# Layer 0's batch ends spread over 40 steps with roots by GpSimd; layer 1's tokens made inside layer 0 and its scan placed at the last value products

## The reference, cut to what matters

```
layer 0 attention (16 heads of 8, per batch):
  scores = (q k' + c2p + p2c) / scale      # c2p, p2c: by relative position
  out    = softmax(scores) v  @ Wo + bo + xn
  out    = (out - mu) * rsqrt(var + 1e-7) * ln_scale + ln_bias
layer 0 ffn:       xn @ sign(weight)'
layer 1 attention (min-GRU, forward and backward over 512 tokens):
  z = sigmoid(xn Wz + bz);  g = xn Wh + bh
  h_t = (1 - z_t) h_(t-1) + z_t G(g_t);    out = [h_f, h_b] @ W_out + b_out
layer 1 ffn (8 experts, 2 per token, 64 places per expert and group of 512):
  probs = softmax(xn @ w_router); two best experts, place = rank in the group
  dispatch -> gelu(. wi[e]) wo[e] -> combine weighted with probs
```

## Time and profile before

| what | us |
|---|---|
| median of 3 runs | 2280.51 (2279.85 to 2285.18) |
| profiled execution | 2277.15 |
| its span, first to last instruction | 2275.3 |
| PE busy / DVE / ACT / POOL | 1944.4 / 1763.7 / 1430.5 / 1223.2 |
| mean granted TensorE clock | 0.960 of full speed |
| main loop of layer 0, first to last add | 74.5 to 920.9 |
| last value products of layer 0 | 925.2 to 928.8 |
| layer 1's first gate product | 975.4 |
| layer 1's first dispatch mask | 1047.3 |

### The profile page before, as it was taken

One profiled execution on the slowest core, in us unless ns is written; L12 is line 12 of the kernel. 1 busy time (PEld: TensorE's weight loads), 2 busy tenths in 40 slices (PEclk: granted clock), 3 DMA queues, 4 the chain that ended last, 5 costly groups with the idle time before them and its releaser, 6 DMA issues.

```text
span 2275.3 us, 38965 instructions
## 1 busy us (share of the span) xinstructions
PE 1944.4 (85%) x13526; PEld 1473.7 (65%) x13526; DVE 1763.7 (78%) x4099; ACT 1430.5 (63%) x2795; POOL 1223.2 (54%) x1028
## 2 busy tenths in 40 slices
PE   3799898888989898587996999999998468788898
PEld 2566565666666666464683878777876345566797
DVE  7688888888888888457187888888887699873586
ACT  2578777777878777344235666666665257765575
POOL 3777677777777775148053445444543466426400
PEclk9999999999999999789997999999999689999999
DMA  3988788888878786201000000000001000003000
GB/s 105 306 304 303 249 294 274 288 268 278 284 271 281 278 300 227 85 1 35 3 6 1 1 1 1 1 1 1 1 1 31 0 0 1 1 1 98 24 2 38
DMA packets 73877, 264.15 MB, mean 116 GB/s; under 512 B 12273, under 2 KB 32241, under 8 KB 73169
## 3 DMA queue, kind: packets, MB, share of 16 engines
q1 hardware_dynamic: 72304, 254.31, 33.2%
q10 hardware_dynamic: 1376, 7.34, 0.8%
HBM read 140.30 MB, written 121.31 MB: 115 GB/s over the span
## 4 chain that ended last, share of the span: by engine, by line
PE 38%; DVE 8%; ACT 6%; POOL 2%; issue 2%; DMA 0%; POOLq 0%; ACTq 0%; DVEq 0%; SPq 0%
PE PS L157 10%; PE PS L161 7%; PE PS L163 7%; PE PS L162 7%; PE PS L326 7%; ACT AR L167 3%; ACT L167 2%; DVE AR L181 1%; DVE DR L181 1%; DVE PT L181 1%; ACT AR L171 1%; ACT PT L171 1%; DVE AR L185 1%; DVE AR L200 1%; DVE AR L193 1%
## 5 line engine op out<-in xcount | busy, mean ns | idle before, releaser
L167 ACT ACTIVATE AR<-PS,AR 128x512 f32<-128x512 f32 x1008 | 686.6, 688 | 286.8 <-DVE AR L193 178.8
L193 DVE TENSOR_REDUCE AR<-PS 128x1 f32<-128x512 f32 x896 | 616.4, 688 | 119.3 <-PE PS L163 100.5
L326 PE MATMUL PS<-ident,AR 128*128 128x128 f32 x3816 | 584.6, 277 | 86.1 <-ACT AR L171 38.6
L157 PE MATMUL PS<-AR 128*9 128x512 f32 (+8 forms) x4190 | 503.5, 360 | 93.0 <-DVE AR L181 32.9
L326 PEld LDWEIGHTS PS<-ident,AR 128*128 128x128 f32 x3816 | 435.0, 142 | 200.6 <-issue 71.2
L181 POOL TENSOR_TENSOR AR<-AR 128x512 f32<-128x512 f32 (+6 forms) x310 | 380.6, 1244 | 226.9 <-DVE AR L181 97.0
L157 PEld LDWEIGHTS PS<-AR 128*9 128x9 f32 (+5 forms) x4190 | 288.8, 133 | 298.4 <-DVE AR L181 130.1
L171 ACT ACTIVATE AR<-PS 128x512 f32<-128x512 f32 (+3 forms) x612 | 356.4, 587 | 91.8 <-PE PS L326 47.7
L176 POOL TENSOR_SCALAR AR<-AR 128x512 f32<-128x512 f32 x144 | 245.4, 1704 | 293.2 <-DVE AR L1596 219.4
L171 ACT ACTIVATE PT<-PS 128x512 fp32r<-128x512 f32 x320 | 191.5, 599 | 208.3 <-PE PS L326 171.5
L181 DVE TENSOR_TENSOR PS<-PS,AR 128x192 f32<-128x192 f32 (+1 forms) x512 | 201.7, 394 | 118.0 <-PE PS L534 112.0
(11 more groups left out here) (157 smaller groups left out, 3001.9 us busy)
## 6 DMA issues: line engine op xcount, KB each, us to landing
scr<-AR SPq DMA_DIRECT2D x128, 800.0 KB, 4.3
XN<-scr SPq DMA_DIRECT2D x85, 768.0 KB, 6.6
AR<-scr SPq DMA_DIRECT2D x43, 768.0 KB, 6.5
AR<-qsc SPq DMA_DIRECT2D x96, 192.0 KB
qsc<-AR SPq DMA_DIRECT2D x96, 128.0 KB, 3.4
AR<-in_wgu SPq DMA_DIRECT2D x16, 256.0 KB, 3.2
X<-in_x ACTq DMA_DIRECT2D x1, 2048.0 KB, 8.5
AR<-in_wi ACTq DMA_DIRECT2D x1, 2048.0 KB, 8.2
```

What stands on the lines that cost most here:

```text
L157: return pe.e.matmul(out, lhsT, rhs, start=start, stop=stop)
L167: return ac.e.activation(out, in_, func, bias=bias, scale=scale, accum_out=accum)
L193: return dv.e.tensor_reduce(out, in_, AX.X, ALU.max, negate=True)
L326: return pe.e.transpose(out, in_, ident[0:k, 0:k])
```

## The change

Layer 0: the ends get one set of places and three new pieces. Step 41 norms T1, step 44 makes the tokens of the batch before last for layer 1 (XR), step 49 transposes them into B_M, and ScalarE copies them into XT in place of layer 0's own. The root is a power of -0.5 on GpSimd over 8 columns: four for T1, four for the batch before's X. newton3 refines it in three operations. The main loop ends 14 steps earlier, and the last batch's end moves into layer 1's units (END0). Layer 1 has no norm stage: its XN are made by `normed`, four scalings a unit. Its small weights are asked for at the last but one group's value products, wi and wo2 by SP after the last end. The router's products stand in groups of four tiles between units 5 and 13; the choice runs in two parts, 28 tiles in units 12 to 14 and the last 4 in unit 15; the ranks' products stand behind unit 15, the exponential behind the last sigmoid, the normalisation of PROB behind the masks. AR loses 36 columns to NY; waits and counts of layers 2 and 3 are renumbered.

```
+def newton3(dv, y, v, tmp):
+    dv.step(stt(dv, y, tmp, -0.5, tmp, ALU.mult, ALU.mult))
+    dv.settle()
+    dv.step(tt(dv, y, y, v, ALU.mult))
+    dv.settle()
+    return stt(dv, y, y, 1.5, tmp, ALU.add, ALU.mult)
...
-        STEPS0 = 4 * NBH + 28
+        STEPS0 = 4 * NBH + 14
-        AHEAD = {"q": 1, "k": 3, "far": 13, "g0": 15, "v": 35}
+        AHEAD = {"q": 1, "k": 3, "far": 13, "g0": 15, "v": 51}
-        ENDS = [{"heads": 17, "ct": 19, "mo": 29, "sw": 31, "root": 34, "norm": 36, "sum": 38, "last": 48}] * NB
-        ENDS += [{"heads": 14, "ct": 16, "mo": 18, "sw": 19, "root": 21, "norm": 22, "sum": 23, "last": 25}]
+        ENDS = {"heads": 17, "ct": 19, "mo": 29, "stats": 32, "root": 34, "norm": 41, "tokens": 44, "sw": 45, "sum": 47, "xt": 49,
+                "last": 57}
...
+            if 2 <= b < NB and r == ENDS["xt"]:
+                uses.append(("xt", b - 2, 0))
...
+                elif what == "xt":
+                    pe.wait_ge(tn_n, 2 * b + 3)
+                    for q in range(4):
+                        ins = tr(pe, ps[:, q * 128:q * 128 + 128], XR[:, q * 128:q * 128 + 128])
...
                 elif k == 1:
-                    dv.wait_ge(m_mm, number["sw", b, 0] + 1)
-                    tt(dv, X[:, xs, :], ps, X[:, xs, :], ALU.add).then_inc(m_dv, 1)
                     dv.wait_ge(*emptied[number["mo", b, 0]])
                     dv.settle()
                     stats(dv, lmv, lst, T1)
                     dv.settle()
-                    ts(dv, lv, lmv[:, :, 1], 1e-7, None, ALU.add).then_inc(tn_v, 1)
+                    if b:
+                        dv.step(ts(dv, lv[:, 4:8], NMV[:, 4 * b - 4:4 * b, 1], 1e-5, None, ALU.add))
+                    ts(dv, lv[:, 0:4], lmv[:, :, 1], 1e-7, None, ALU.add).then_inc(tn_v, 1)
...
-                    dv.step(newton(dv, ly, lv, ltmp))
+                    w = 8 if b else 4
+                    dv.step(newton3(dv, ly[:, 0:w], lv[:, 0:w], ltmp[:, 0:w]))
...
+                elif k == 3:
+                    dv.wait_ge(m_mm, number["sw", b, 0] + 1)
+                    tt(dv, X[:, xs, :], ps, X[:, xs, :], ALU.add).then_inc(m_dv, 1)
+                elif k == 5:
+                    if b:
+                        done = 6 * min(b + 3, NB)
+                        dv.wait_ge(sp_p, done)
+                        dv.wait_ge(sp_a, done)
+                        dv.settle()
+                        dv.step(dv.e.tensor_copy(NY[:, 4 * b - 4:4 * b], ly[:, 4:8]))
+                        for i in range(4 * b - 4, 4 * b):
+                            ins = ts(dv, XR[:, i % 4 * 128:i % 4 * 128 + 128], X[:, i, :], NMV[:, i, 0:1], ly[:, 4 + i % 4:5 + i % 4],
+                                     ALU.subtract, ALU.mult)
+                        ins.then_inc(tn_n, 1)
...
-                        act(ac, ltmp, lv, ACT.Sqrt).then_inc(tn_q, 1)
+            def root(b):
+                w = 8 if b else 4
+                po.wait_ge(po_init, HALF_0)
+                po.wait_ge(tn_v, b + 1)
+                tt(po, ltmp[:, 0:w], lv[:, 0:w], minus_half[:, 0:w], ALU.pow).then_inc(tn_q, 1)
...
+        LAST = NB - 1
+        END0 = {"heads": 0, "ct": 1, "mo": 2, "stats": 3, "sw": 4, "root": 4, "norm": 5, "sum": 6, "xt": 8, "last": 8, "root7": 9,
+                "norm7": 10, "tr7": 11}
+        ROUTER = {5: (0, 4), 6: (4, 8), 7: (8, 12), 8: (12, 16), 9: (16, 20), 10: (20, 24), 11: (24, 28), 13: (28, 32)}
         def l1_sp(sp):
+            sp.wait_ge(pv_mm, 4 * NB - 1)
...
+            after_l0(sp)
+            for dst, name in ((wi, "wi"), (wo2, "wo2")):
+                sp.e.dma_start(dst, a[name]).then_inc(ld[1], 16)
...
-        def l1_pe(pe):
-            norm_pe(pe, 1, lambda c: 4 + c + 1)
+        def l1_pe(pe, small_mm):
             pe.wait_ge(ld[1], NL1)
-            pe.wait_ge(n_xt, 16)
+            pe.wait_ge(s_ex, 4 * NBH)
+            pe.wait_ge(to_a, 4 * NBH)
...
+            for u in range(16):
+                unit(u)
+                for what, b, g in (("heads", LAST, 3), ("ct", LAST, 0), ("mo", LAST, 0), ("sw", LAST, 0), ("xt", LAST - 1, 0)):
+                    if u == END0[what]:
+                        small_mm((what, b, g))
+                if u in ROUTER:
+                    tokens((ROUTER[u][1] - 1) // 4)
+                    for i in range(*ROUTER[u]):
+                        ins = mm(pe, PS[:, 7 if i >= 4 * LAST else 6, i * 8:i * 8 + 8], XT[:, i * 128:i * 128 + 128], router, True, True)
...
+                if u % 2 and u >= 3:
+                    scan_out(u // 2 - 1)
+                if u == END0["tr7"]:
...
+                        ins = tr(pe, PS[:, 7, q * 128:q * 128 + 128], XN[:, 4 * LAST + q, :])
...
+            trail()
             scan_out(NB - 1)
...
+            def normed(b):
+                dv.settle()
+                for i in range(4 * b, 4 * b + 4):
+                    ins = ts(dv, XN[:, i, :], X[:, i, :], NMV[:, i, 0:1], NY[:, i:i + 1], ALU.subtract, ALU.mult)
+                ins.then_inc(xn_dv, 1)
...
+            ROUTE = {12: ((0, first),), 13: ((1, first),), 14: ((2, first),), 15: ((0, last), (1, last), (2, last))}
             for u in range(16):
                 gate(u)
                 if u:
                     scan(u - 1)
                 if u % 2 and u >= 3:
                     scan_out(u // 2 - 1)
-                route(u)
+                for k, sl in ROUTE.get(u, ()):
+                    route(k, sl)
+                if u < LAST:
+                    normed(u)
...
             scan(15)
+            counted()
             scan_out(7)
```

More of the change, by code:

```diff
@@ L419, in program @@
             order += small(u)
+        order += [("heads", NB - 1, 3), ("ct", NB - 1, 0), ("mo", NB - 1, 0), ("sw", NB - 1, 0), ("xt", NB - 2, 0)]
         number, emptied, n_ac, n_dv = {}, [], 0, 0
@@ L588, in l0_pe @@
                     pv(G, r // 2)
+            return small_mm
         def l0_dv(dv):
@@ L927, in l0_po @@
                     split(b + 1, k // 2, k % 2)
-                if b >= 1 and r == ENDS[b]["sum"]:
+                if 1 <= b < NB and r == ENDS["root"]:
+                    root(b - 1)
+                if 1 <= b < NB and r == ENDS["sum"]:
                     tail(b - 1)
+            return root, tail
         def l0_sp(sp):
@@ L1038, in after_l0 @@
             en.wait_ge(p_w, 2 * NBH)
+            en.wait_ge(to_a, 4 * NBH)
+            en.wait_ge(s_ex, 4 * NBH)
+            en.wait_ge(pv_mm, 4 * NB)
         A1 = Arena(nc, AR, ar_at)
         names1 = ["wz_f", "wh_f", "wz_b", "wh_b"]
+        H_, A_ = [A1.take(512) for _ in range(4)], [A1.take(512) for _ in range(3)]
+        PRI, PROB = A1.take(NT, 8), A1.take(NT, 8)
+        assert 2 * 2048 <= A1.top
         w1 = [A1.take(128) for _ in names1]
@@ L1047, in program @@
         router, trile, iota, rev = A1.take(8), A1.take(128), A1.take(64), A1.take(8)
[L1048 to L1051 removed]
+        assert A1.top <= 4 * 2048 and 4 * NB % 2 == 0 and PTN == 6
+        ones128, v7, tmp7 = A1.take(128), A1.take(4), A1.take(4)
         L, L2, E1, E2, W_ = (A1.take(NT, 8) for _ in range(5))
         m8, s8 = A1.take(NT), A1.take(NT)
[L1054 removed]
+        Z0, *ZG = [A1.take(512) for _ in range(6)]
         Z_, G_ = [Z0, *ZG[:2]], ZG[2:]
         zg_at = A1.top - 5 * 512
[L1057 removed]
+        assert A1.top <= PTN * 2048
+        wi, wo2 = A1.take(8, 512), A1.take(8, 4, 128)
         XIN = A1.take(8, 8, 64)
@@ new lines, in route, with counted @@
+                    first_max(E2[:, sl], L2[:, sl], sl).then_inc(rt_dv, 1)
+            def counted():
+                dv.wait_ge(rt_mm, 3)
+                dv.wait_ge(rt_dv, 2)
+                dv.settle()
+                ps = PS[:, 7, :].rearrange("p (k n e) -> p k n e", k=2, e=8)
+                dv.step(tt(dv, E1, E1, ps[:, 0], ALU.mult))
+                dv.step(tt(dv, E2, E2, ps[:, 1], ALU.mult))
+                dv.settle()
+                dv.step(tt(dv, PRI, E1, E2, ALU.max))
+                dv.settle()
+                ts(dv, PRI, PRI, -1.0, None, ALU.add).then_inc(rt_dv, 1)
@@ L1283, in l1_dv @@
                     scan_out(u // 2 - 1)
-                route(u)
+                for k, sl in ROUTE.get(u, ()):
+                    route(k, sl)
+                if u < LAST:
+                    normed(u)
+                if u == END0["heads"]:
+                    heads_out(LAST, 3)
+                if u == END0["mo"]:
+                    tail(LAST, 0)
+                if u == END0["stats"]:
+                    tail(LAST, 1)
+                if u == END0["norm"]:
+                    tail(LAST, 2)
+                    tail(LAST, 3)
+                    tail(LAST, 5)
+                if u == END0["last"]:
+                    tail(LAST, 4)
+                    dv.settle()
+                    ts(dv, v7, NMV[:, 4 * LAST:NT, 1], 1e-5, None, ALU.add).then_inc(tn_v, 1)
+                if u == END0["norm7"]:
+                    dv.wait_ge(tn_v, NB + 1)
+                    dv.wait_ge(tn_q, NB + 1)
```

(11 more changed lines are left out.)

280 lines of the change are left out of this document (140 added, 140 removed).

## The result

The changed kernel takes 2268.68 us (median of 4 runs, 2266.0 to 2271.58) where the kernel before, on the same chip, takes 2280.18: a ratio of 0.9945, interval 0.9924 to 0.9966. It is 11.5 us faster; 44 were forecast. The profiled execution took 2271.58 us, its span is 2269.7.

| us | before | forecast | after |
|---|---|---|---|
| layer 0, first to last add | 846.4 | 831.4 | 858.2 |
| last add to layer 1's first dispatch mask | 126.3 | 96.7 | 108.7 |
| first mask to the end | 1228.1 | 1228.1 | 1228.6 |

The account below looks back on a forecast made before the run. No single engine was the bound: DVE and TensorE alternate. Profiled 2277.15 us less 15 (layer 0's ends) and 29.6 (earlier scan) gave 2232.6, or 2236 on the median of the runs, range 2218 to 2258.

Parts of the forecast that it names:

- steps 40 to 43 of part 1: Layer-0 quarter taking the norm, four scalings and the tokens: 2.8 us of new work less 0.96 spare, 6.13 to 8.0.
- part 1: Layer 0's batch ends spread over 40 steps: 2.2 us gained per batch, 15 us for seven (6 to 27).
- The table loads: Layer 0, steps 34 and 35: ScalarE's two loads round the root go, within steps 32 to 35 falling 10.39 to 6.2.
- Part 2: Layer 1's scan begins at 928.8, right after the last value products: masks near 1017.7, 29.6 us gained (19.6 to 44).
- Rival (e): Layer 1's early start fails because weights or tokens hold unit 0: at most 2.3 us lost, counted inside the forecast.
- The walk: Layer 1's scan followed on the DVE, unit by unit: work to 1003, 8.7 us of waits, so 1011.7 before two extras.
- 3 us for three such meetings: Layer 1: DVE scans beside GpSimd take 2.27 us instead of 1.21; 3 us added, ends 0 to 8.
- The power: GpSimd's root of eight columns at step 34, wanted at 41: 0.6 us, ends 0.2 to 2.4.
- rival (d): GpSimd's nine roots delay the bands the DVE's add waits for; at 8 us each 2294 us. Chance 0.05.
- (a): Work alone counts in layer 0, which gains 0 to 3 us: 2249 us. Chance 0.18.
- (b): Layer 1's scan pays for its guests: waits double, both extras reach their ends, part 2 gains 11: 2254 us. Chance 0.13.
- The hidden things: Router's exponential and table beside the rank products, PROB's normalisation (1.4 us) beside the experts, expert weights asked 50 us ahead.

Follow-up runs that it names:

- the experiment: The changed kernel plus seven 512-column products into a free bank, keeping TensorE busy ahead of the rank products: 2261.1 us, ratio 0.9926 to the kernel before.

## Why the prediction was wrong

The direction was right, and so was most of the place. The size, 11.5 us instead of 44, fell outside the range; two of the three things that I had said would show the forecast wrong did so, the quarter at 40 (10.3, over 9) and the stretch from the last value products to the first mask (940.3 to 1041.10, 100.8 us, just over 100).

**The step that failed first: steps 40 to 43 of part 1.** "2.8 us, less the 0.96 that the quarter has to spare: 8.0." The bare part of this holds: with the norm alone and unheld the quarter takes 6.86, where 6.13 + 1.65 - 0.96 is 6.8. What failed was taking each instruction at the shortest duration the trace shows it with. Measured 10.3 = 8.0 + 0.86 (norm held) + 1.58 (tokens held), within 0.2. That is 2.3 us over the forecast in five of the seven batches, 4.3 in the last, where three of the four token scalings are held, and 1.5 in the first that carries an end: some 17 of the 27 us by which layer 0 missed. The same in small at steps 28 to 31: the "one small operation more" takes 0.66 us, because it starts beside GpSimd's band product of 443.86 and ends with it, and that quarter took 8.8 instead of 7.9.

```profile
445.04 0.66 DVE L176 TENSOR_SCALAR AR<-NMV 128x4 f32<-128x4 f32 x1
445.61 0.16 DVE L176 TENSOR_SCALAR AR<-AR 128x4 f32<-128x4 f32 x1
```

I had the evidence. The earlier trace rows show a hold and the prediction says "exactly while GpSimd's band product runs"; the earlier trace rows show a scan at 2.27 beside GpSimd. I used the first as a stall that goes away and the second as an extra for three scans, and never as a rule for the 60 new or moved scalings and what goes with them. A rival "each new scaling meets GpSimd as often as GpSimd is busy" would have been easy to price: GpSimd is busy 0.75 of a batch, and a meeting costs the rest of an instruction of 0.6 to 1.8 us.

**The later quarters of part 1.** Steps 44 to 47 and 48 to 51 were forecast at 6.9 and 5.9 and took 7.5 and 7.0 on the mean; 60 to 63 went from 5.55 to 6.06 and 36 to 39 from 6.12 to 6.72, which I had not looked at; 52 to 59 came out 1.1 us better than forecast. Leaving the tokens out takes 1.0 off the first of these; the second stays at 7.0 without them and with them on ScalarE, so it is the transposes, their copy and the projection. The run with the old places parts these: it has transposes and copy in that quarter but not the projection, and takes 5.5 there where the kernel before takes 5.0. So some 0.4 us are theirs and most of the rest is the projection's, though there the statistics of X stand in the quarter too.

**The table loads.** The sum counted the two loads as a pure stall, and quarter 32 to 35 did fall, to 5.5 where 6.2 was forecast. But the old kernel without the loads gains nothing until the norm moves, so the fall comes from moving the norm, and the value weights' output with it, away. That the spreading is worth 14.2 us or a little more doesn't confirm the 15 of the sum: those also had the loads in them and the tokens against them. What the sum missed is the price of the new work at its new places.

**Part 2.** The early start came as forecast: tokens, weights and exponentials in time, the first gate product as soon as TensorE is free, no table load before it, the eleven loads issued between 927 and 932. Rival (e) is out. The walk was 11.9 us too short (88.9 against 100.8). "3 us for three such meetings" counted scans only; there were 13 held scalings with 11 us of excess. How much of it reached the end is not settled: moving all the scalings to ScalarE returned 4.6, thinning GpSimd's own queue 4.8, and each of the two also changes something else. "For the low clock 3 us" was 5.7 by the rows (15.7 against 9.99), and 6.9 by the experiment, since the output product behind the ranks was slow too; its ground, idle time ahead of the group, was right.

**The power.** 1.65 us for eight columns and 1.04 for four, not 0.6: inside my ends, nearer the upper one. It ran seven steps before its use, and newton3 starts without idle time before it in every batch; rival (d) is out. Rivals (a) and (b) each name a part of what happened (new work shows in full; guests of the scan double their price), but (a) gave layer 0 0 to 3 us of gain and it lost 11.8, (b) gave the second part 11 us and it gained 17.6, and neither had the hold as a cost of layer 0. The hidden things I had named stayed hidden: mask to end moved by 0.5 us.

## What to carry to other kernels

Before giving the DVE new instructions that work in SBUF alone (products of two tensors, scalings, copies), look at what GpSimd runs at that place: each costs its own time plus the rest of the GpSimd instruction it meets, and the place, to one step, can be worth more than the instruction. Where ScalarE has idle time, a scale and shift is cheaper there: so in layer 0 (21 us), hardly in layer 1 (4.6), where the sigmoids queue behind it. Where GpSimd's instruction is released by the DVE itself, put the DVE's own work one step behind it. And an instruction that takes five times its usual time in the old trace is a rule to be applied to the change, not a stall to be credited to it.

## What the runs showed of the hardware beyond what I expected

- A hold covers one GpSimd instruction, not GpSimd's queue, and two if the DVE arrives in the last moment of the first (the token scaling of 465.61, 0.06 us before the first band product's end, waited out the second): of four back-to-back scalings up to four are held in turn (5.14 us for 1.11), the DVE getting one in between two GpSimd instructions.
- It goes both ways: the GpSimd product of layer 1 takes 2.11 us behind a 1.22 us scan that began 0.17 us before it (2.11 to 2.19 in 15 of the 16 units), and one of its shape takes 1.05 in layer 0 where no such DVE instruction runs.
- BATCH_NORM_STATS, one SBUF input, was not held beside the same band product that held the scaling behind it (four took 0.86 us from 443.73 on, beside GpSimd's 443.86 to 445.67). A copy of 128x4, 0.16 us unheld, took 0.51 in the run with the tokens at 45.
- ScalarE's scale and shift of 128x128 takes 477 to 526 ns, longer than the DVE's unheld 335, with or without GpSimd beside it, and in layer 0 is still the cheaper place.
